# A graph transformer kernel on one core: another order in the first iterations, and the last chunk in pieces

## What is computed

```
h = relu(layernorm(x)); x = x + attention0(h, adj)      # 8 heads of 32, q/k/v/out weights and biases
h = relu(layernorm(x)); x = x + attention1(h, adj)      # masked attention, then o + layernorm(o)
h = relu(layernorm(x)); x = x + graph_attention(h, adj) # elu(att @ hW + beta * hW)
h = relu(layernorm(x)); x = x + gated_recurrence(h, adj):
    for _ in range(3):
        a  = adj @ h                                    # in_mat = out_mat = adj
        z  = sigmoid([a, a] w3 + b3 + h u3 + c3)
        r  = sigmoid([a, a] w4 + b4 + h u3 + c3)
        hv = tanh([a, a] w5 + b5 + (r * h) u5 + c5)
        h  = (1 - z) * h + z * hv
```

## Time and profile before

| | before |
|---|---|
| median of 3 executions | 1524.75 us (1520.08 to 1526.09) |
| profiled execution | 1525.95 us, span 1524.2 us |
| PE busy | 1463.7 us (96%), 18840 matmuls |
| DVE busy | 1244.6 us (82%) |
| ACT busy | 991.5 us (65%) |
| POOL busy | 534.8 us (35%) |
| mean granted TensorE clock | 0.986 |

### The profile page before, as it was taken

One profiled execution on the slowest core, in us unless ns is written; L12 is line 12 of the kernel. 1 busy time (PEld: TensorE's weight loads), 2 busy tenths in 40 slices (PEclk: granted clock), 3 DMA queues, 4 the chain that ended last, 5 costly groups with the idle time before them and its releaser, 6 DMA issues.

```text
span 1524.2 us, 45691 instructions
## 1 busy us (share of the span) xinstructions
PE 1463.7 (96%) x18840; PEld 1233.9 (81%) x18840; DVE 1244.6 (82%) x2510; ACT 991.5 (65%) x1792; POOL 534.8 (35%) x622
## 2 busy tenths in 40 slices
PE   5899999899899998799999999999999999999997
PEld 4789989799798887588888888888888887888885
DVE  4777888888899999788888788888888888888676
ACT  4666667577677776666666666666666666666553
POOL 2676777567777887411111111111101111111000
PEclk9999999999999999899999999999999999999998
DMA  8200000012322235100000000000000000000000
GB/s 263 85 3 0 0 0 1 7 26 44 58 55 55 55 64 78 29 1 1 29 2 2 30 1 1 30 1 1 30 1 1 30 1 1 29 2 1 29 1 28
DMA packets 36827, 40.96 MB, mean 27 GB/s; under 512 B 11856, under 2 KB 31824, under 8 KB 36688
## 3 DMA queue, kind: packets, MB, share of 16 engines
q0 software_dynamic: 4608, 16.78, 5.9%
q1 hardware_dynamic: 32080, 22.10, 4.9%
HBM read 13.71 MB, written 8.39 MB: 14 GB/s over the span
## 4 chain that ended last, share of the span: by engine, by line
PE 87%; DVE 7%; POOL 2%; ACT 2%; issue 2%; DMA 0%; DVEq 0%; POOLq 0%; ACTq 0%
PE ring L99 40%; PE scores L99 27%; PE scores L1589 3%; PE ring L1408 3%; PE scores L1372 2%; PE ring L1448 2%; PE ring L1629 2%; PE ring L1419 1%; PE ring L1573 1%; PE ring L1701 1%; PE ring L1531 1%; POOL s L534 1%; PE ring L1542 1%; DVE total L993 1%; DVE stats L955 1%
## 5 line engine op out<-in xcount | busy, mean ns | idle before, releaser
L534 POOL TENSOR_TENSOR s<-s,mx 128x512 f32<-128x512 f32 x128 | 137.4, 1092 | 49.4 <-DVE mx L989 49.4
L540 POOL TENSOR_TENSOR s<-s,rtotal 128x512 f32<-128x512 f32 x128 | 131.4, 1064 | 35.9 <-DVE rtotal L995 35.7
L600 POOL TENSOR_TENSOR r_var_eps<-r_mean_var,eps 128x4 f32<-128x4 f32 x16 | 8.1, 509 | 377.1 <-DVE r_mean_var L1146 377.1
L684 ACT ACTIVATE s<-s 128x512 f32<-128x512 f32 x128 | 78.3, 643 | 75.1 <-POOL s L534 75.1
L1275 DVE TENSOR_TENSOR rhp_lo<-r,rhp_hi 128x1024 fp32r<-128x1024 f32 x48 | 58.8, 1226 | 72.8 <-ACT rhp_hi L865 72.8
L984 DVE SCALAR_TENSOR_TENSOR s<-scores,mask 128x512 f32<-128x512 f32 x128 | 87.2, 681 | 35.4 <-PE scores L1372 35.4
L884 ACT ACTIVATE hv<-scores,bias 128x512 f32<-128x512 f32 x96 | 66.2, 689 | 58.0 <-PE scores L99 58.0
L847 ACT ACTIVATE r<-r,bias_half 128x512 f32<-128x512 f32 x96 | 64.4, 717 | 59.6 <-DVE r L1249 59.6
L858 ACT ACTIVATE later_w<-ring 128x512 f32<-128x512 f32 x64 | 34.8, 595 | 99.9 <-PE ring L1629 99.9
L696 ACT ACTIVATE pT<-ring 128x512 f32<-128x512 f32 x128 | 66.1, 602 | 45.4 <-PE ring L1408 45.4
L989 DVE TENSOR_REDUCE mx<-s 128x8 f32<-128x512 f32 x128 | 87.9, 686 | 4.4
(11 more groups left out here) (288 smaller groups left out, 5108.6 us busy)
## 6 DMA issues: line engine op xcount, KB each, us to landing
x<-beta_less_one POOLq DMA_DIRECT2D x16, 512.0 KB, 4.7
x<-o POOLq DMA_DIRECT2D x16, 512.0 KB, 6.6
out_x<-x SPq DMA_DIRECT2D x16, 512.0 KB, 2.9
x<-in_x SPq DMA_DIRECT2D x1, 6144.0 KB, 26.5
later_w<-in_L_gnn_w_w SPq DMA_DIRECT2D x3, 512.0 KB, 6.7
x<-in_x SPq DMA_DIRECT2D x2, 512.0 KB, 5.1
x<-in_x SPq DMA_DIRECT2D x1, 1024.0 KB, 8.1
stage<-in_L_gnn_w_qkv SPq DMA_DIRECT2D x3, 256.0 KB, 3.1
```

What stands on the lines that cost most here:

```text
L534: pool.tensor_tensor(sr, sr, mx[:, r, :].unsqueeze(2).to_broadcast([P, CT * 2, N]), ALU.subtract).then_inc(s_shifted, 1)
L540: pool.tensor_tensor(sr, sr, rtotal[:, r, :].unsqueeze(2).to_broadcast([P, CT * 2, N]), ALU.mult).then_inc(p_ready, 1)
L684: act.activation(s[:, par, r, :, :, :], s[:, par, r, :, :, :], ACT.Exp).then_inc(p_exp, 1)
```

## The change

Five edits, on all engines but with no change of what is computed:

1. Start of TensorE: 48 transposes of the identity into a bank of scores that is not yet in use ahead of the first iteration, and ten more in iteration -1 behind the transposes of chunk 0's rows (`keep_clock`).
2. Iteration 0: TensorE transposes chunk 1's rows ahead of chunk 0's scores; the bias product moves from the end to between q and k. ScalarE and VectorE get a `first_body` of their own: the high part of wo and `bv_rows` behind the high rows of chunk 1, the first exponential between the copies of q and k; masks ahead of the bias row and of the statistics of chunk 2.
3. Iteration 1: the probability transposes and their copies are split in two pairs with the rows between them; the statistics of chunk 3 move behind the masks, the low part of wo from iteration -1 to here.
4. GpSimd in iterations 0 and 1: the norm moves behind the four shifts.
5. Last chunk: half 47 (`closing`) also makes r*h and its parts, one feature bank at a time, ahead of the z sums and of chunk 14's last add; w5, u5, tanh, the three steps and the transposes go in four pieces of 256 columns (q is the half of the rows, m the feature bank; `last_banks`); the last transposes go to `high`, and the last store is two of two tiles each.

```diff
--- before.py
+++ after.py
@@ -401,6 +401,7 @@
...
+                self.closing = fixed and self.n == GROUPS * HALVES - 1
...
@@ -446,6 +447,10 @@
...
+
+        def last_banks(q, m):
+
+            return (high[:, 2 + m, 0:D] if q == 0 else ring[:, m, 0:D]), slice(q * D, (q + 1) * D)
...
@@ -493,10 +498,14 @@
...
                         .then_inc(adj_loaded, 16)
                 dst = out.rearrange("b n d -> (b n) d").rearrange("(t p) d -> p t d", p=P)
-                with sp.Fori(0, CHUNKS) as c:
+                with sp.Fori(0, CHUNKS - 1) as c:
                     sp.wait_ge(left, c * 2 + 2)
                     sp.dma_start(dst[:, bass.ds(c * CT, CT), :], x[:, bass.ds(c * CT, CT), :]).then_inc(stored, 16)
-                sp.wait_ge(stored, 16 * CHUNKS)
+                for q in range(2):
+                    cut = slice((CHUNKS - 1) * CT + 2 * q, (CHUNKS - 1) * CT + 2 * q + 2)
+                    sp.wait_ge(left, (CHUNKS - 1) * 2 + q + 1)
+                    sp.dma_start(dst[:, cut, :], x[:, cut, :]).then_inc(stored, 16)
+                sp.wait_ge(stored, 16 * (CHUNKS + 1))
 
             @block.gpsimd
...
@@ -568,7 +577,9 @@
...
                 def body(i, par, lay):
-                    norms(i, par, lay)
+                    first = isinstance(i, int) and i in (0, 1)
+                    if not first:
+                        norms(i, par, lay)
...
@@ -588,6 +599,8 @@
...
                         shift(i, par, 3)
+                    if first:
+                        norms(i, par, lay)
...
@@ -724,11 +737,33 @@
...
+                def first_body():
+                    split_high(1)
+                    act.wait_ge(w_loaded[3], 16)
+                    act.activation(parts[0]["o"].hi[:], stage[:, 3, :, :], ACT.Copy).then_inc(w_hi_ready, 1)
+                    act.activation(bv_rows[:], col_bias[:, 2, :].unsqueeze(2).to_broadcast([P, FT, P]), ACT.Copy)\
+                        .then_inc(bv_spread, 1)
+                    copy_projection(1, 0, qT, 0)
+                    exponential(0, 0, 0)
+                    copy_projection(1, 1, kT, 0)
+                    for r in range(1, R):
+                        exponential(0, 0, r)
+                    copy_v(1, 1)
+                    normalise(0, 0, 0)
+
                 def body(i, par, lay):
-                    if exists(i - 1):
+                    if isinstance(i, int) and i == 0:
+                        first_body()
+                        return
+                    second = isinstance(i, int) and i == 1
+                    if second:
+                        copy_pT(i, range(2))
+                    elif exists(i - 1):
                         copy_pT(i)
                     if exists(i + 1):
                         split_high(i + 1)
+                    if second:
+                        copy_pT(i, range(2, R))
...
@@ -757,11 +792,6 @@
...
-                    if isinstance(i, int) and i == -1:
-                        act.wait_ge(w_loaded[3], 16)
-                        act.activation(parts[0]["o"].hi[:], stage[:, 3, :, :], ACT.Copy).then_inc(w_hi_ready, 1)
-                        act.activation(bv_rows[:], col_bias[:, 2, :].unsqueeze(2).to_broadcast([P, FT, P]), ACT.Copy)\
-                            .then_inc(bv_spread, 1)
...
@@ -847,10 +877,27 @@
...
+                def close(n):
+                    for m in range(FT):
+                        act.wait_ge(rh_done, n + m)
+                        act.activation(rhp.hi[:, m, :], r[:, m, :], ACT.Copy).then_inc(rh_hi_ready, 1)
+                    for m in range(FT):
+                        act.wait_ge(z_added, (n - 1) * FT + m + 1)
+                        act.activation(z[:, m, :], z[:, m, :], ACT.Tanh, bias=bias_half[:, 0, m:m + 1], scale=0.5)\
+                            .then_inc(z_done, 1)
+                    for q in range(2):
+                        for m in range(FT):
+                            bank, cut = last_banks(q, m)
+                            act.wait_ge(hv_ready, (n - 1) * FT + 2 * q + m + 1)
+                            act.activation(hv[:, m, cut], bank, ACT.Tanh, bias=bias[:, 2, m:m + 1]).then_inc(hv_done, 1)
+
...
                         begin(s)
+                        return
+                    if s.last:
+                        close(n)
                         return
...
@@ -1081,11 +1128,26 @@
...
+                def first_body():
+                    rows_low(1)
+                    for r in range(R):
+                        mask_and_max(0, 0, r, 0)
+                    dve.wait_ge(bias_product, 1)
+                    dve.tensor_tensor(out_bias[0][:], out_bias[0][:], scores[:, 0, 0:D], ALU.add)\
+                        .then_inc(bias_ready, 1)
+                    x_stats(2, 0)
+                    for r in range(R):
+                        sums(0, 0, r)
+
                 def body(i, par, lay):
-                    opening = isinstance(i, int) and i <= 0
+                    if isinstance(i, int) and i == 0:
+                        first_body()
+                        return
+                    opening = isinstance(i, int) and i == -1
+                    second = isinstance(i, int) and i == 1
                     if opening:
                         rows_low(i + 1)
-                    if exists(i + 2) and not (opening and i == -1):
+                    elif exists(i + 2) and not second:
                         x_stats(i + 2, lay)
...
@@ -1102,6 +1164,8 @@
...
+                    if second:
+                        x_stats(i + 2, lay)
                     if exists(i - 1):
                         o_low(i - 1)
...
@@ -1109,13 +1173,11 @@
...
+                    if second:
+                        split_low(0, [3])
...
-                    if isinstance(i, int) and i == 0:
-                        dve.wait_ge(bias_product, 1)
-                        dve.tensor_tensor(out_bias[0][:], out_bias[0][:], scores[:, 0, 0:D], ALU.add)\
-                            .then_inc(bias_ready, 1)
...
@@ -1128,7 +1190,6 @@
...
-                        split_low(0, [3])
...
@@ -1215,12 +1276,43 @@
...
-                def leave(c):
+                def leave(c, psum=ring, bank=2):
...
-                        dve.tensor_tensor(xc, xc, ring[:, 2 + q, :].rearrange("p (t d) -> p t d", t=2),
+                        dve.tensor_tensor(xc, xc, psum[:, bank + q, :].rearrange("p (t d) -> p t d", t=2),
...
+                def close_rh(s):
+                    n = s.n + 1
+                    old = h[s.me]
+                    for m in range(FT):
+                        dve.wait_ge(r_done, s.n * FT + m + 1)
+                        dve.scalar_tensor_tensor(r[:, m, :], r[:, m, :], 1.0, old[:, m, :], ALU.add, ALU.mult)\
+                            .then_inc(rh_done, 1)
+                    for m in range(FT):
+                        dve.wait_ge(rh_hi_ready, n + m)
+                        dve.tensor_tensor(rhp.lo[:, m, :], r[:, m, :], f32(rhp.hi[:, m, :]), ALU.subtract)\
+                            .then_inc(rh_lo_ready, 1)
+
+                def close(s):
+                    n = s.n
+                    old, new = s.h_before(), h[s.other]
+                    dve.wait_ge(z_done, n * FT)
+                    for q in range(2):
+                        for m in range(FT):
+                            cut = last_banks(q, m)[1]
+                            count = (n - 1) * FT + 2 * q + m + 1
+                            dve.wait_ge(hv_done, count)
+                            dve.tensor_tensor(hv[:, m, cut], hv[:, m, cut], old[:, m, cut], ALU.subtract)\
+                                .then_inc(hv_minus_h, 1)
+                            dve.wait_ge(hv_minus_h, count)
+                            dve.scalar_tensor_tensor(hv[:, m, cut], z[:, m, cut], 1.0, hv[:, m, cut], ALU.add, ALU.mult)\
+                                .then_inc(hv_gated, 1)
+                            dve.wait_ge(hv_gated, count)
+                            dve.scalar_tensor_tensor(new[:, m, cut], hv[:, m, cut], 0.5, old[:, m, cut],
+                                                     ALU.mult, ALU.add).then_inc(h_done, 1)
+                    leave(s.leaves, high, 0)
 
                 def update(s, m):
...
@@ -1300,6 +1395,8 @@
...
+                    if s.closing:
+                        close_rh(s)
...
@@ -1475,13 +1572,38 @@
...
+                def keep_clock(bank, times):
+
+                    for _ in range(times):
+                        pe.transpose(bank[:, 0:P], ident[:], ident[:])
+
+                def bias_of_values():
+                    pe.wait_ge(w_loaded[3], 16)
+                    pe.wait_ge(bv_spread, 1)
+                    pe.wait_ge(s_masked, 1)
+                    for k in range(FT):
+                        last = pe.matmul(scores[:, 0, 0:D], bv_rows[:, k, :], stage[:, 3, k, :],
+                                         start=(k == 0), stop=(k == FT - 1))
+                    last.then_inc(bias_product, 1)
+
                 def body(i, par, lay):
```

(63 more changed lines are left out.)

4 lines of the change are left out of this document (2 added, 2 removed).

## The result

| | before | after |
|---|---|---|
| median, us (lowest to highest, runs) | 1524.18 (1520.08 to 1526.09, 4) | 1504.9 (1503.79 to 1505.45, 4) |
| profiled execution, us; span | 1525.95; 1524.2 | 1503.79; 1502.0 |
| mean granted clock | 0.986 | 0.991 |

The ratio is 0.9876, 95% interval 0.9861 to 0.9891: 1.2% faster. The pair of profiled executions is 22.2 us apart where the sum said 13.2.

The account below looks back on a forecast made before the run. TensorE was taken as the bound over most of the run, with gains only where it waits or runs slowly. 2.3 + 7.0 + 3.9 = 13.2 us off 1525.95 gave 1512.75, against the median 1511.55; forecast 1512 us, range 1506 to 1518.5.

Parts of the forecast that it names:

- (a): Start of TensorE: dummy transposes raise the clock before the first projection; gain 2.3 us, other end 0.7 us lost.
- won back by the ten that follow: Start: if standing still 2.6 us loses the higher rate, ten dummies behind the first real transposes restore it; within 2.3 us.
- Rival 1: Start: the dummies do not hold the clock, 0.7 us lost instead of 2.3 gained; 1515 us, chance 0.22.
- (b): Iterations 0 and 1: the other order starts later work earlier, carried to the end; gain 7.0 us, ends 4 and 8.
- six handovers: Iterations 0 and 1: handovers taken as free; at 0.5 us each the reordering gains 4 us instead of 7.0.
- the lower end: Iterations 0 and 1: reordering gains only 4 us, if each handover taken as free costs 0.5 us.
- (c): Last chunk: r*h earlier, work in smaller pieces, smaller last store; gain 3.9 us, ends 2.5 and 4.7.
- the upper end: Last chunk: gain 4.7 us, if the u5 pieces keep the rate up through the last transposes.
- Rival 2: Whole program: moving 9 us against whatever decides the clock gives part of the gain back; 1520 us, chance 0.13.
- Rival 3: GpSimd: the late norm is carried on through the remaining 29 iterations, 0.75 us each; 1534 us, chance 0.03.

Follow-up runs that it names:

- the last run with 28: Kernel after with 28 dummy transposes at the start instead of 48, and 40 already met waits behind them: 1507.91 us, ratio 0.9888.
- 116 in time: Kernel before with met waits filling 116 instructions, spread over three places where TensorE waits anyhow: 1520.74 us, ratio 0.9976.
- 116 ahead: Kernel before with 232 met waits, filling 116 instructions, at the start of TensorE's queue: 1522.2 us against 1524.43, ratio 0.999.
- dummies alone: Kernel before with only the 58 dummy transposes added: 1516.72 us, ratio 0.9952.
- no dummies, with and without filling: Kernel after without its 58 dummy transposes: with 232 met waits in their place 1509.66 us, without them 1515.35 us.
- kernels at 116 or 117: Five kernels, the one after included, whose loops stand 116 or 117 instructions behind their place in the kernel before: 1504.9 to 1522.2 us.

## Why the prediction was wrong

**The sum's terms were right.** (a) was put at 2.3 us and measured 2.7 (55.22 to 52.56). The dummies ended at 9.9 instead of 9.5, the rate was held at 12.09, and the ten are part of what holds it: without them 1.6 us go. The other way that the prediction left open, a lost rate "won back by the ten that follow", is in the last run with 28: TensorE stands still for 5.38 us, the eight real transposes take 1.94, the ten behind them 1.98, and the first 512-column products run at the higher rate. What the ten would do with no dummies ahead of them no run shows. Rival 1 fell. The sentence of the Trainium skill that stood against this part, in its page "TensorE: Matmul & The Clock Gate", section on PE-mode transpose, is not borne out: the 48 transposes end 7.9 us after they began, where 48 at the lower rate's 0.21 us would take 10, and the eight behind them run at 1.09 us after nothing but transposes.

(b) was put at 7.0 and measured 7.1 (62.34 to 55.23 alone). The chain through GpSimd was read rightly: its first shift of iteration 1 at 39.52 (forecast 39.8), value products 41.80 (42.1), scores of chunk 2 at 52.56 (53.0). None of the six handovers cost what the lower end allowed.

(c) was put at 3.9 and measured 4.3 in the trace, 3.9 by median alone. The twelve small steps cost 0.42 each as the bias row had said. The last four transposes took 0.66 us, not 1.05: as the upper end had it, the rate was still up, behind waits of 1.24 and 1.79 us where the kernel before has one of 3.69. That the u5 pieces are what keeps it up is argued, not shown. The last store saved 0.9 instead of 0.7.

**The step that failed** is the end of (b): "From iteration 2 TensorE is the bound again and the shift is carried to the end". It was: 14.1 us of forecast terms measured against 13.2. But it took for granted that the middle costs the same wherever its code stands. I costed the 58 dummies by the time in which they run, and not by what they push along in TensorE's program. In the medians, 1524.18 - 1504.9 = 19.3 less 14.1 leaves 5.2 us. Four pairs of runs say what the place is worth, each as its gain in the median less what its start changed by the profiles: 3.5 us (116 in time: 3.0 and 0.5), 5.4 (116 ahead: 2.2 and 3.2), 6.4 (dummies alone: 7.7 less 1.3), 8.6 (no dummies, with and without filling: 5.7 and 2.9). The 5.2 lie among them. Why they differ is open: the 116 in time and the dummies alone have their loops at the same place and the same work behind it in the same order, and are still about 2 us apart in the middle (1432.6 and 1430.3). Part of it is that code at the old place pauses differently in each execution: the times of one kernel differ there by 5 to 8 us (1512.9 to 1520.7 without dummies), those of the kernels at 116 or 117 by 2 to 4. In the profiled pair the middle gives 8.1 us, 6.3 of them at the pauses; the profiled execution of before was one of its slower ones.

The rows were there. The waits of the kernel before have the line "ring L1448 <- issue" with 4.3 us in two waits, the largest idle time of TensorE in the middle without a cause, and I passed it over since it was not in the change's way. Rival 2 had the right place, "the whole program moves against whatever decides", with the wrong sign and the wrong thing: not the time by which it moves, but the number of instructions.

Rival 3 fell: no iteration became longer; from the scores of chunk 3 to those of chunk 4 it is 17.06 us after, and 18.37 before, a pause of 1.02 us in it.

## What to carry to other kernels

An instruction that is added to an engine's queue moves all code behind it, and its price is not only its own time: a change of a few dozen instructions can gain or lose 3 to 8 us here with the same work. So look in the profile of before for idle time with the releaser "issue" in code that runs for the first time, and at the head of a long loop's passes, and when a part is tested without its instructions, leave as many in their place; else the part gets the credit for the place. For a forecast, put that time in as a term with both signs: what pauses now may go, and the new places may pause.

## What the runs showed of the hardware

- TensorE pauses in code that runs for the first time: 30 pauses up to 430 us, of up to 2.51 us, all at place 222 to 226 of a block of 256 instructions. It also pauses at the head of each later pass of a loop of about 1,940 (0.19 to 0.84 us). The granted clock was low behind a longer one (0.66 in the 5 us from 391 before). The Trainium skill, page "Runtime: NRT & Kernel Launch", section "Instruction fetch mechanics", states that instructions are refilled in blocks of 16 KiB, 256 instructions, and that TensorE holds 2048. The trace agrees in the packets of 16 KB and in the loop of about 1,450 instructions, which is fetched once; the loop of about 1,940, below 2048 too, is fetched again on every pass (10 packets in 110 us). It calls the cost of crossing a block mostly hidden; with rows of 2.08 and 2.25 us in this kernel, the measurement decides against that for stretches of small matmuls.
- A met wait is not free: 116 instructions of them ahead of the first transposes took until 14.6 us, and 256 until 29.9, 0.11 us each between the two.
- Transposes alone raised TensorE's rate; after standing still for 2.18 us it was kept (1.09 us for eight), and for 2.69 partly lost (1.31 for eight, then 0.63 a product behind another 1.90 of standing still). Eighteen transposes that began at the lower rate, at 12.13 in the last run with 28, brought it up again by 15.60 (first product 0.48 us, the next 0.40).
